# Two of twelve products with C per phase on GpSimd, and the small-argument logarithm by its remainder, in a GRU plus selective-scan kernel

## The chip, the cores and the metric

The kernel runs on one core of a Trainium2 chip. The metric is the time of the whole program on the device in microseconds (us), as the median of several runs; lower is better. A core has TensorE (PE), VectorE (DVE), ScalarE (ACT), GpSimd (POOL) and SyncE (SP, which here only issues DMAs). Each engine works through its own list of instructions in order, and they meet at semaphores.

## The reference, cut to what matters

The input is 32 images of 14 x 14 positions (T = 196) and 384 channels. A group norm and a GRU over the 196 positions come first, then a group norm and a selective scan in four directions:

```python
dts, Bs, Cs = jnp.split(x_dbl, [R, R + N], axis=2)        # N = 16 states
dts = jax.nn.softplus(einsum(dts, dt_projs_w) + dt_projs_b)
dA = jnp.exp(d_t[..., None] * As)                          # per channel and state
h = h * dA + (d_t * u_t)[..., None] * B_t[:, :, None, :]
y = jnp.einsum('bkcn,bkn->bkc', h, C_t)
```

The four y are added, normalised over the channels, gated with silu(z) and projected.

## The kernel before, in words

The GRU and the projections of all images fill the first 1,020 us. The change touches only what follows: a loop over 16 pairs of images (`PAIRS`), in each of which four directions (the phases `st` = 0 to 3, which the change's title calls phases and the prediction stages) are done one after the other. A stage has twelve groups `g`. A group holds a block of 128 partitions x 784 elements (`GC`): four runs of 196 positions, each for one state and a part of the channels. One group passes through all engines:

- GpSimd, `drive` (L484): delta\*u times B, into one of six buffers `hb` (`RING` = 6), so group g uses the buffer of group g - 6 and waits until that one was summed (the semaphore `reduced`). B comes by DMA, replicated over the partitions, in three chunks of four groups.
- ScalarE, `decays` (L950): exp(delta\*A) in two halves into three PSUM banks (`DEC` = 3), so a half waits for the scan three halves before.
- VectorE, `scan` (L767): two scan instructions of 392 elements, in place in `hb`; then `read_out` (L782): the product with C, in place. C lies in PSUM banks 3 and 4, put there by TensorE.
- TensorE, `spread` (L1229): four matmuls that replicate the C rows of a group into banks 3 and 4; `reduce` (L1237): matmuls with the identity that add the group into the sum over the states, banks 5 and 6.

In TensorE's list (`pair`, L1302) iteration g waits for the product of group g - 1, spreads C of group g and reduces group g - 1; projections for the next stage and the tail of the image pair before are hung on behind: `dt_proj` at g = 0 and 2, a wait for ScalarE's reading of it (`dt_read`) at g = 3 and 4, `centre_hw` at (0,3), `centre_wh` at (0,4), `var` at (1,4), `out_proj` with `residual` at (3,3) and (3,5), `bc_proj` at g = 8 and 9.

In GpSimd's list (`pair`, L513) drive(g) is followed at g = 4 by `resid_of` (L448), at g = 8 by `low_parts` (L454), and at g = 10 and 11 by the five steps of `delta_step` (L460), which make delta and delta\*u of the next stage. In stage 2 `normed` (L498) stands behind drive(4), ahead of `resid_of`, and `gated` (L502) behind drive(7): both belong to the pair of images before. ScalarE's `mid_parts` (L922, at g = 3) waits for `resid_of`, and its `affine` (L992, at (2,2)) for `normed`.

The softplus is max(x,0) + log(1+e) with e = exp(-|x|). Before, for e under 0.022 a series takes the place of what the plain logarithm loses: ScalarE makes it by a square and a copy, GpSimd by two products and differences, and VectorE's `choose` (L790, once a stage, after group 8) picks it. The order of all lists is written out by hand; no planner is at work. SyncE issues the loads, each behind the wait that frees its target (`pair`, L341).

Of the kernel before, what the change touches and what calls it, by code (L numbers as in the profile page):

```python
# [39 lines left out]
CHUNK = 16 * T  # L40
EPS = 1e-5
UNROLL = 32
A_LOG_MAX = 88.72
SMALL = 0.022
# [5 lines left out]
def build(nc, x_seq, x_pair, wx, wh, bx, bh, wp, win, par, xproj, dtproj, wout, out):  # L50
# [4 lines left out]
    b_by_image = nc.dram_tensor("b_by_image", [K4, 2, N, T], F32)  # L55

    with ExitStack() as ctx:
# [18 lines left out]
        ident = sb("ident", [128, 128])  # L76
        sel = sb("sel", [96, N, 3, 128], BF16)
# [15 lines left out]
        series_bias = sb("series_bias", [128, 1])  # L93
# [40 lines left out]
        def carve(cols):  # L134
# [19 lines left out]
        poly = carve(TC)  # L154
# [26 lines left out]
            "dt_ready", "dt_read", "soft_step", "series_step", "choice_ready", "log_ready", "delta_ready", "du_ready",  # L181
# [6 lines left out]
            "b_spilled", "b_chunk0", "b_chunk1", "b_chunk2", "skipped")}  # L188
# [20 lines left out]
        def group_aps(g):  # L209

            if g < 8:
                return (lambda a: a[:, 0:T2].unsqueeze(1).broadcast_to([128, 2, T2]),
                        lambda bank: ps[:, bank:bank + 2, 0:T2],
                        lambda a: a.rearrange("p (m c) -> p m c", m=2))
            return (lambda a: a[:, T2:TC].unsqueeze(1).unsqueeze(1).broadcast_to([128, 2, 2, T]),
                    lambda bank: ps[:, bank:bank + 2, 0:T2].rearrange("p m (q t) -> p m q t", q=2),
                    lambda a: a.rearrange("p (m q t) -> p m q t", m=2, q=2))

# [12 lines left out]
        def _(sp):  # L231
# [65 lines left out]
            def spill_b(P, k):  # L297
# [3 lines left out]
                sp.dma_start(b_by_image[k].rearrange("i n t -> (i n) t"), xdbl[0:2 * N, 0:T]).then_inc(s["b_spilled"], 16)  # L301

# [14 lines left out]

            spill_b(0, 0)
            for j in range(3):
                spread_b(0, 0, j, True)  # L320
            spill_xc(PAIRS - 1)
# [19 lines left out]
            def pair(i, head, last):  # L341
                for st in range(K4):
# [5 lines left out]
                    if st == 1 and not last:  # L348
                        next_x(i)
                    if ahead:  # L350
                        spread_b(P1, k1, 1)
                    if st == 3 and not head:
# [17 lines left out]
        def _(pool):  # L370
# [89 lines left out]
            def delta_step(n, P, k, b, early=False):  # L460

                if n == 0:
                    pool.wait_ge(s["soft_step"], P * 4 + 3)
                    pool.tensor_tensor(poly, poly, soft, ALU.mult).then_inc(s["series_step"], 1)  # L464
                elif n == 1:
                    pool.wait_ge(s["soft_step"], P * 4 + 4)
                    pool.wait_ge(s["series_step"], P * 2 + 1)
                    pool.tensor_tensor(poly, poly, lnp, ALU.subtract).then_inc(s["series_step"], 1)  # L468
                elif n == 2:
                    pool.wait_ge(s["series_step"], P * 2 + 2)  # L470
                    pool.tensor_tensor(lnp, lnp, relu, ALU.add).then_inc(s["log_ready"], 1)  # L471
                elif n == 3:
                    pool.wait_ge(s["choice_ready"], P + 1)
# [3 lines left out]
                    pool.tensor_tensor(delta[b], lnp, poly, ALU.add).then_inc(s["delta_ready"], 1)  # L477
# [6 lines left out]
            def drive(P, st, g, G, early):  # L484
# [7 lines left out]
                if not early:  # L492
                    pool.wait_ge(s["reduced"], G - (RING - 1))
# [12 lines left out]

            pool.wait_ge(s["xc_loaded"], 16)
            resid_of(0, 0)
            low_parts(0, 0)
            for n in range(5):  # L510
                delta_step(n, 0, 0, 0, True)

            def pair(i, head, last):  # L513
                for st in range(K4):
# [3 lines left out]
                    for g in range(GRP):  # L518
                        drive(P, st, g, i * (K4 * GRP) + (st * GRP + g), head and st * GRP + g < RING)
                        if (st, g) == (2, 4) and not head:  # L520
# [10 lines left out]
                        if g >= 10:  # L531
                            for n in (0, 1, 2) if g == 10 else (3, 4):
# [11 lines left out]
        def _(dve):  # L544
            dve.memset(series_bias[:, :], -(3.0 ** 0.5) / 4.0).then_inc(s["const_ready"], 1)
# [123 lines left out]
            dve.wait_ge(s["const_ready"], 2)  # L669
# [112 lines left out]
            def read_out(st, g, G):  # L782
# [4 lines left out]
                dve.wait_ge(s["c_ready"], G + 1)  # L787
                dve.tensor_tensor(h, h, bank(3), ALU.mult).then_inc(s["readout_ready"], 1)  # L788

            def choose(P):  # L790

                dve.wait_ge(s["series_step"], P * 2 + 2)
                dve.scalar_tensor_tensor(poly, soft, SMALL, poly, ALU.is_lt, ALU.mult  # L793
                    ).then_inc(s["choice_ready"], 1)

            def pair(i, head, last):
                for st in range(K4):
                    for g in range(GRP):
# [7 lines left out]
            choose(0)  # L806
# [7 lines left out]
        def _(act):  # L814
# [98 lines left out]
            def read_bc(P, st, first=False):  # L913
                act.wait_ge(s["bc_ready"], P * 2 + 2)
                if not first:
                    act.wait_ge(s["dt_ready"], P * 2)
                    act.wait_ge(s["resid_ready"], P)
                    act.wait_ge(s["b_spilled"], P * 48)
                act.activation(xdbl[:, :], ps[:, 7, 0:T2], ACT.Copy).then_inc(s["xdbl_ready"], 1)
# [17 lines left out]
            def series(P, part):  # L937

                if part == 0:
# [3 lines left out]
                    act.activation(poly, soft, ACT.Square, scale=3.0 ** -0.5, bias=series_bias[:, 0:1]  # L943
                        ).then_inc(s["soft_step"], 1)
# [143 lines left out]
        def _(pe):  # L1088
# [39 lines left out]
            pe.wait_ge(s["const_ready"], 2)  # L1128
# [108 lines left out]
            def reduce(st, g):  # L1237
# [4 lines left out]
                opens, closes = st % 2 == 0 and g in (0, 8), st % 2 == 1 and g in (7, 11)  # L1242
# [59 lines left out]
            def pair(i, head, last):  # L1302
                for st in range(K4):
# [3 lines left out]
                    for g in range(GRP):  # L1307
# [4 lines left out]
                        if not opening:  # L1312
                            pe.wait_ge(s["readout_ready"], G)
                        spread(g, st)
                        if not opening:
# [4 lines left out]
                            reduce(*((st, g - 1) if g else ((st - 1) % K4, GRP - 1)))  # L1320

# [55 lines left out]
            pe.wait_ge(s["readout_ready"], PAIRS * K4 * GRP)  # L1377
# [60 lines left out]
```

## Time and profile before

| | |
|---|---|
| median of 3 runs | 3240.07 us (3240.0 to 3241.2) |
| the profiled execution's own time | 3240.27 us |
| its span | 3238.3 us |
| PE busy | 2779.2 us, 86% |
| DVE busy | 2672.7 us, 83% |
| POOL busy | 2243.0 us, 69% |
| ACT busy | 1824.2 us, 56% |
| DMA, mean over the span | 119 GB/s |

Shares over the span mix two programs, the GRU and the scan loop. The loop on VectorE runs from 1022.79 us to 3203.93 us, 2181.14 us; in it DVE is busy for 2141.79 us (98%), POOL for 1952.29 (90%), PE for 1816.78 (83%) and ACT for 1589.99 (73%). A timeline row gives the start, the duration, the engine, the line, and how many instructions were merged in it; what stands in brackets is the idle time before it and who ended it. A row's duration includes its way out of the engine's pipeline, so the distance between two starts is what one instruction costs its engine.

### The profile page before, as it was taken

How to read it: one execution, taken by the hardware profiler on the slowest of the kernel's cores; microseconds unless marked ns; L12 is line 12 of the kernel's file. 1: busy time of each engine (PE TensorE's matmuls, PEld its weight loads, DVE VectorE, ACT ScalarE, POOL GpSimd, SP SyncE). 2: the span in 40 equal slices, each digit the busy share in tenths (PEclk: the TensorE clock that was granted, in tenths of full speed). 3: DMA queues.
4: the chain of work that ended last, by engine and by line, in shares of the span. 5: the costliest groups of instructions: out<-in, count | busy, mean ns of one | idle time of the engine just before them, and what ended most of it. 6: DMA issues, size and time to landing. Idle time of an engine off the chain costs nothing.

```text
span 3238.3 us, 101526 instructions
## 1 busy us (share of the span) xinstructions
PE 2779.2 (86%) x39496; PEld 2070.2 (64%) x39496; DVE 2672.7 (83%) x4226; ACT 1824.2 (56%) x3872; POOL 2243.0 (69%) x1878
## 2 busy tenths in 40 slices
PE   4999999999996788888888888888888888888886
PEld 4999999986664555555555555565555655656554
DVE  6444444445776999999999999999999999999995
ACT  1111111112224677777777777777777777777773
POOL 5333333320005989989899898888989898898983
PEclk9999999999997999999999999999999999999999
DMA  5000000002334555545545555455454554555541
GB/s 199 0 0 0 0 0 0 0 5 97 112 112 140 156 156 153 153 156 149 177 140 163 159 144 169 141 160 174 134 170 149 157 163 140 162 161 155 162 146 46
DMA packets 57085, 385.29 MB, mean 119 GB/s; under 512 B 10100, under 2 KB 15060, under 8 KB 31700
## 3 DMA queue, kind: packets, MB, share of 16 engines
q1 hardware_dynamic: 57044, 384.79, 38.8%
q8 instruction: 20, 0.33, 0.0%
q14 instruction: 21, 0.17, 0.0%
HBM read 352.64 MB, written 32.11 MB: 119 GB/s over the span
## 4 chain that ended last, share of the span: by engine, by line
DVE 30%; PE 25%; issue 23%; POOL 16%; ACT 3%; DMA 1%; DVEq 1%; POOLq 0%; SPq 0%; ACTq 0%
DVE arena L776 15%; PE ps L1112 10%; PE ps L1121 9%; POOL arena L495 9%; DVE arena L779 9%; PE ps L1108 2%; DVE arena L793 1%; DVE conv_out L203 1%; POOL arena L471 1%; POOL arena L464 1%; POOL arena L468 1%; DVEq L773 1%; DMA x_in<-x_pair 1%; POOL arena L477 1%; POOL arena L482 1%
## 5 line engine op out<-in xcount | busy, mean ns | idle before, releaser
L1244 PE MATMUL ps<-arena,ident 128*128 128x392 f32 (+1 forms) x4096 | 1163.0, 417 | 0.9 <-DVE arena L788 0.9
L963 ACT ACTIVATE ps<-arena,abias,a 128x390 f32<-128x390 f32 x1024 | 690.0, 677 | 317.4 <-DVE arena L779 179.8
L788 DVE TENSOR_TENSOR arena<-arena,ps 128x784 f32<-128x784 f32 x768 | 745.7, 971 | 38.2 <-PE ps L1234 12.8
L1244 PEld LDWEIGHTS ps<-arena,ident 128*128 128x128 f32 x4096 | 682.8, 191 | 143.9 <-DVE arena L788 1.2
L776 DVE TENSOR_TENSOR_SCAN arena<-ps,arena 128x392 f32<-128x392 f32 x768 | 702.6, 956 | 7.4 <-POOL arena L495 6.3
L779 DVE TENSOR_TENSOR_SCAN arena<-ps,arena 128x392 f32<-128x392 f32 x768 | 702.6, 956 | 0.0
L1234 PE MATMUL ps<-arena,sel 96*128 96x196 bf16 x3072 | 391.6, 250 | 355.7 <-DVE arena L788 355.7
L1234 PEld LDWEIGHTS ps<-arena,sel 96*128 96x128 bf16 x3072 | 227.5, 97 | 665.0 <-DVE arena L788 630.7
L967 ACT ACTIVATE ps<-arena,abias,a 128x195 f32<-128x195 f32 x1024 | 477.7, 505 | 254.2 <-DVE arena L776 139.8
L495 POOL TENSOR_TENSOR arena<-arena 128x784 f32<-128x784 f32 x256 | 472.7, 1851 | 102.6 <-PE ps L1244 97.3
L495 POOL TENSOR_TENSOR arena<-arena,wx_sb 128x784 f32<-128x784 f32 x256 | 465.4, 1850 | 14.4 <-POOL arena L482 13.7
L495 POOL TENSOR_TENSOR arena<-arena,wh_sb 128x784 f32<-128x784 f32 x256 | 467.9, 1850 | 0.0
L422 POOL COPY arena<-h_t 128x96 f32 x196 | 71.6, 365 | 421.5 <-DVE h_t L667 421.5
L1112 PE MATMUL ps<-wx_sb,x_cur 128*32 128x96 f32 x14112 | 333.2, 248 | 0.0
L1121 PE MATMUL ps<-wh_sb,h_t 128*32 128x96 f32 x14112 | 330.6, 247 | 0.0
L1112 PEld LDWEIGHTS ps<-wx_sb,x_cur 128*32 128x32 f32 x14112 | 290.9, 110 | 23.1 <-issue 0.2
L652 DVE TENSOR_TENSOR rh<-r_gate,ps 128x96 f32<-128x96 f32 x196 | 49.8, 254 | 308.6 <-PE ps L1121 308.6
L1121 PEld LDWEIGHTS ps<-wh_sb,h_t 128*32 128x32 f32 x14112 | 296.9, 110 | 4.9
L843 ACT ACTIVATE r_gate<-ps 128x96 f32<-128x96 f32 x196 | 49.0, 250 | 394.0 <-PE ps L1121 394.0
L439 POOL TENSOR_TENSOR grstd<-gsum,neg_half 128x6 f32<-128x6 f32 x16 | 21.2, 1323 | 240.3 <-DVE gsum L723 240.3
L1214 PE MATMUL ps<-arena,bc_w 128*128 128x196 f32 x768 | 150.0, 332 | 1.5 <-ACT arena L935 0.8
L1214 PEld LDWEIGHTS ps<-arena,bc_w 128*128 128x128 f32 x768 | 133.6, 192 | 19.6 <-ACT arena L935 1.4
(175 smaller groups left out, 3295.4 us busy)
## 6 DMA issues: line engine op xcount, KB each, us to landing
wx_sb<-b_by_state SPq DMA_DIRECT2D x64, 1568.0 KB, 6.3
wh_sb<-b_by_state SPq DMA_DIRECT2D x64, 1568.0 KB, 6.3
arena<-b_by_image SPq DMA_DIRECT2D x128, 784.0 KB, 9.1
arena<-x_seq SPq DMA_DIRECT2D x4, 2352.0 KB, 15.9
x_in<-x_pair SPq DMA_DIRECT2D x16, 588.0 KB, 4.2
x_dram<-x SPq DMA_DIRECT2D x16, 588.0 KB, 2.8
x<-x_dram SPq DMA_DIRECT2D x16, 588.0 KB, 10.0
out<-xhat SPq DMA_DIRECT2D x16, 588.0 KB, 2.8
```

Source lines behind the costliest of these rows:

```text
L422: pool.tensor_copy(tok(t), h_t[:, p, :]).then_inc(s["hist_done"], 1)
L495: pool.tensor_tensor(view(hb[(st * GRP + g) % RING]), dux(du[b]), view(src), ALU.mult).then_inc(s["drive_ready"], 1)
L776: dve.tensor_tensor_scan(h, ps[:, bank, 0:HALF_C], h, 0.0, ALU.mult, ALU.add).then_inc(s["scan_done"], 1)
L779: dve.tensor_tensor_scan(h[:, ::-1], ps[:, bank, 1:HALF_C + 1][:, ::-1], h[:, ::-1], 0.0, ALU.mult, ALU.add).then_inc(s["scan_done"], 1)
L788: dve.tensor_tensor(h, h, bank(3), ALU.mult).then_inc(s["readout_ready"], 1)
L963: ins = act.activation(r, src, ACT.Exp, scale=a01[:, c:c + 1], bias=abias01[:, c:c + 1])
L967: ins = act.activation(r[:, m, :], delta[b][:, T2 + lo:T2 + lo + T - 1], ACT.Exp, scale=a2[:, c:c + 1], bias=abias2[:, c:c + 1])
L1112: mm = pe.matmul(ps[32 * j:32 * j + 32, bank + p, 0:CJ], x_cur[:, p, 32 * k:32 * k + 32], wx_sb[:, k, j, lo:lo + CJ], start=False, stop=False)
L1121: mm = pe.matmul(ps[32 * j:32 * j + 32, bank + p, at:at + CJ], h_t[:, 1 - p, 32 * k:32 * k + 32], wh_sb[:, k, j, lo:lo + CJ], start=False, ...
L1214: mm = pe.matmul(ps[:, 7, bc * T:(bc + 1) * T], bc_w[:, k, bc, tile, :], x[:, tile * T:(tile + 1) * T], start=(tile == 0), stop=(tile == 2))
L1234: mm = pe.matmul(ps[:, 3 + m // 2, m % 2 * T:m % 2 * T + T], sel[:, n, kind, :], rhs, start=True, stop=True)
L1244: mm = pe.matmul(ps[:, 5 if g < 8 else 6, 0:cols], ident[:, :], h[:, m * cols:(m + 1) * cols], start=(opens and m == 0), stop=(closes and ...
```

## The change

Groups 2 and 6 of every stage lose VectorE's `read_out`; GpSimd multiplies them instead (`pool_read`), three drives after their own, with a copy of C that DMA wrote to DRAM and spread over the partitions (`spread_c`). TensorE doesn't spread C for them, and reduces them two iterations later than before: at g = 5 and 9. The order of the reductions becomes 0, 1, 3, 4, 2, 5, 7, 8, 6, 9, 10, 11, and `drive` counts `reduced` by that order. The softplus takes its logarithm of w = 1 + e as rounded, and adds the remainder e - (w - 1): two copies and a Ln on ScalarE, four steps on GpSimd, none on VectorE. The diff, cut to its core:

```diff
+POOL_READS = (2, 6)
+DVE_READS = GRP - len(POOL_READS)
+READ_LEAD = 3
+BEHIND = 2
@@ sync, spill_b
+                for q, g in enumerate(POOL_READS):
+                    for img in range(2):
+                        sp.dma_start(c_by_state[k][q, :, img, :], xdbl[N * img + 2 * g:N * img + 2 * g + 2, T:T2]
+                                     ).then_inc(s["c_spilled"], 16)
+            def spread_c(P, k, first=False):
+                sp.wait_ge(s["c_spilled"], (P + 1) * (32 * len(POOL_READS)))
+                if not first:
+                    sp.wait_ge(s["pool_read"], P * len(POOL_READS))
+                rows = c_by_state[k].rearrange("q n i t -> (q n i t)").unsqueeze(0)
+                sp.dma_start(c_chunk[:, :], rows.broadcast_to([128, len(POOL_READS) * GC])).then_inc(s["c_chunk_in"], 16)
@@ sync, pair
                     if ahead:
                         spread_b(P1, k1, 1)
+                    if ahead and max(POOL_READS) + READ_LEAD >= 8:
+                        spread_c(P1, k1)
@@ gpsimd, delta_step
                 if n == 0:
                     pool.wait_ge(s["soft_step"], P * 4 + 3)
-                    pool.tensor_tensor(poly, poly, soft, ALU.mult).then_inc(s["series_step"], 1)
+                    pool.tensor_tensor(rest, soft, rest, ALU.subtract).then_inc(s["rest_ready"], 1)
                 elif n == 1:
-                    pool.tensor_tensor(poly, poly, lnp, ALU.subtract).then_inc(s["series_step"], 1)
+                    pool.tensor_tensor(lnp, lnp, rest, ALU.add).then_inc(s["log_ready"], 1)
                 elif n == 2:
-                    pool.tensor_tensor(lnp, lnp, relu, ALU.add).then_inc(s["log_ready"], 1)
-                elif n == 3:
-                    pool.wait_ge(s["choice_ready"], P + 1)
-                    pool.tensor_tensor(delta[b], lnp, poly, ALU.add).then_inc(s["delta_ready"], 1)
+                    pool.tensor_tensor(delta[b], lnp, relu, ALU.add).then_inc(s["delta_ready"], 1)
@@ gpsimd, drive
-                    pool.wait_ge(s["reduced"], G - (RING - 1))
+                    before = st * GRP + g - RING
+                    place = before // GRP * GRP + ORDER.index(before % GRP)
+                    pool.wait_ge(s["reduced"], G - (st * GRP + g) + (place + 1))
@@ gpsimd
+            def pool_read(P, st, g, G):
+                _, _, view = group_aps(g)
+                h = view(hb[(st * GRP + g) % RING])
+                q = POOL_READS.index(g)
+                if q == 0:
+                    pool.wait_ge(s["c_chunk_in"], P * 16 + 16)
+                pool.wait_ge(s["scan_done"], G * 2 + 2)
+                pool.tensor_tensor(h, h, view(c_chunk[:, q * GC:(q + 1) * GC]), ALU.mult).then_inc(s["pool_read"], 1)
@@ gpsimd, pair
                         drive(P, st, g, ...)
+                        if g - READ_LEAD in POOL_READS:
+                            pool_read(P, st, g - READ_LEAD, ...)
-                            for n in (0, 1, 2) if g == 10 else (3, 4):
+                            for n in (0, 1) if g == 10 else (2, 3):
@@ vector, pair
-                        read_out(st, g, G)
-                        if g == 8 and not (last and st == K4 - 1):
-                            choose(i * K4 + (st + 1))
+                        if g not in POOL_READS:
+                            read_out(i * K4 + st, st, g, G)
@@ scalar, series
-                    act.activation(poly, soft, ACT.Square, scale=3.0 ** -0.5, bias=series_bias[:, 0:1]
+                    act.activation(lnp, soft, ACT.Copy, bias=1.0).then_inc(s["soft_step"], 1)
-                    act.activation(poly, poly, ACT.Copy, bias=13.0 / 16.0).then_inc(s["soft_step"], 1)
-                    act.activation(lnp, soft, ACT.Ln, bias=1.0).then_inc(s["soft_step"], 1)
+                    act.activation(rest, lnp, ACT.Copy, bias=-1.0).then_inc(s["soft_step"], 1)
+                    act.wait_ge(s["soft_step"], P * 4 + 3)
+                    act.activation(lnp, lnp, ACT.Ln).then_inc(s["soft_step"], 1)
@@ tensor, pair
-                            pe.wait_ge(s["readout_ready"], G)
-                        spread(g, st)
-                        if not opening:
+                            pe.wait_ge(s["readout_ready"], P * DVE_READS + dve_reads_before(g))
+                        if g not in POOL_READS:
+                            spread(g, st)
+                        if not opening and (g - 1) % GRP not in POOL_READS:
                             reduce(*((st, g - 1) if g else ((st - 1) % K4, GRP - 1)))
+                        if g - 1 - BEHIND in POOL_READS:
+                            r = g - 1 - BEHIND
+                            pe.wait_ge(s["pool_read"], P * len(POOL_READS) + (POOL_READS.index(r) + 1))
+                            reduce(st, r)
```

## Rows read from the trace of the kernel before

**Rows 1.** Windows, stages 1 to 0 of one pair: busy time of each engine.

```profile
1874.71:2011.14 136.43, 114.58 (x584) 79.53 (x584) 133.94 (x150) 100.22 (x192) 122.87 (x79) 1.00 0.52 156
```

**Rows 2.** Waits of the loop: engine and line, releaser, us in total, times, longest.

```profile
POOL arena L495 <- PE ps L1244: 97.3, 89, 2.0
```

**Rows 3.** Timeline of DVE: scans, products with C, the choice L793.

```profile
1874.71 1.83 DVE L779 TENSOR_TENSOR_SCAN arena<-ps,arena 128x392 f32<-128x392 f32 x2
1876.58 0.97 DVE L788 TENSOR_TENSOR arena<-arena,ps 128x784 f32<-128x784 f32 x1
1877.47 1.83 DVE L779 TENSOR_TENSOR_SCAN arena<-ps,arena 128x392 f32<-128x392 f32 x2
...
1933.19 1.40 DVE L793 SCALAR_TENSOR_TENSOR arena<-arena 128x588 f32<-128x588 f32 x1
...
1956.22 0.97 DVE L788 TENSOR_TENSOR arena<-arena,ps 128x784 f32<-128x784 f32 x1 [0.61 <-PE ps L1234]
...
1968.11 0.77 DVE L793 SCALAR_TENSOR_TENSOR arena<-arena 128x588 f32<-128x588 f32 x1
```

**Rows 4.** Timeline of POOL, stage 2 and the first drives of stage 3.

```profile
1887.80 1.87 POOL L495 TENSOR_TENSOR arena<-arena 128x784 f32<-128x784 f32 x1 [0.27 <-PE ps L1244]
...
1912.72 1.42 POOL L500 TENSOR_TENSOR arena<-arena 128x588 f32<-128x588 f32 x1
1914.11 0.54 POOL L451 TENSOR_TENSOR arena<-arena 96x196 f32<-96x196 f32 x1
...
1921.43 1.85 POOL L495 TENSOR_TENSOR arena<-arena 128x784 f32<-128x784 f32 x1
1923.36 0.55 POOL L456 TENSOR_TENSOR arena<-arena 32x196 bf16<-32x196 f32 x1
1924.07 3.67 POOL L495 TENSOR_TENSOR arena<-arena 128x784 f32<-128x784 f32 x2 [0.16 <-POOL arena L456]
1927.69 1.44 POOL L464 TENSOR_TENSOR arena<-arena 128x588 f32<-128x588 f32 x1
1929.21 1.44 POOL L468 TENSOR_TENSOR arena<-arena 128x588 f32<-128x588 f32 x1
...
1934.75 1.43 POOL L477 TENSOR_TENSOR arena<-arena 128x588 f32<-128x588 f32 x1 [0.79 <-DVE arena L793]
1936.35 1.43 POOL L482 TENSOR_TENSOR arena<-arena 128x588 f32<-128x588 f32 x1 [0.16 <-POOL arena L477]
1938.02 7.27 POOL L495 TENSOR_TENSOR arena<-arena,wx_sb 128x784 f32<-128x784 f32 x4 [0.24 <-POOL arena L482]
```

**Rows 5.** Timeline of PE: spread, reduce, and extras at g = 3 and 4.

```profile
1885.87 0.51 PE L1234 MATMUL ps<-arena,sel 96*128 96x196 bf16 x4 [0.90 <-DVE arena L788]
1886.21 1.51 PE L1244 MATMUL ps<-arena,ident 128*128 128x392 f32 x4
1887.56 0.82 PE L1259 MATMUL ps<-arena,avg 128*128 128x392 f32 x2
...
1953.52 0.93 PE L1292 MATMUL ps<-arena,wout 128*128 128x392 f32 x2 [0.50 <-ACT arena L935]
...
1955.61 0.50 PE L1234 MATMUL ps<-arena,sel 96*128 96x196 bf16 x4
...
1987.90 0.92 PE L1259 MATMUL ps<-arena,centring 128*128 128x392 f32 x2 [0.59 <-ACT arena L935]
...
1989.32 0.50 PE L1234 MATMUL ps<-arena,sel 96*128 96x196 bf16 x4
```

**Rows 6.** Timeline of ACT, stage 2, groups 2 to 4.

```profile
1914.18 1.16 ACT L996 ACTIVATE arena<-arena,par 128x392 f32<-128x392 f32 x2 [0.34 <-POOL arena L500]
1915.24 1.26 ACT L963 ACTIVATE ps<-arena,abias,a 128x390 f32<-128x390 f32 x2
1916.53 0.36 ACT L924 ACTIVATE arena<-arena 32x196 bf16<-32x196 f32 x1
...
1918.93 0.42 ACT L935 ACTIVATE arena<-ps,par 128x196 f32<-128x196 f32 x1
```

More of the change, by code:

```diff
@@ L76, in build @@
         ident = sb("ident", [128, 128])
+        c_chunk = sb("c_chunk", [128, len(POOL_READS) * GC])
         sel = sb("sel", [96, N, 3, 128], BF16)
@@ L153, in build @@
         lnp = carve(TC)
-        poly = carve(TC)
+        rest = carve(TC)
         z_fin = carve(TC)
@@ L180, in build @@
             "xc_loaded", "xt_ready", "bc_ready", "xdbl_ready", "resid_ready", "mid_ready", "parts_ready",
-            "dt_ready", "dt_read", "soft_step", "series_step", "choice_ready", "log_ready", "delta_ready", "du_ready",
+            "dt_ready", "dt_read", "soft_step", "rest_ready", "log_ready", "delta_ready", "du_ready",
             "b_ready", "c_ready", "decay_ready", "drive_ready", "scan_done", "readout_ready", "reduced",
@@ L186, in build @@
             "oproj_ready", "o_ready", "out_stored", "fin_z", "fin_x1",
-            "b_spilled", "b_chunk0", "b_chunk1", "b_chunk2", "skipped")}
+            "b_spilled", "b_chunk0", "b_chunk1", "b_chunk2", "skipped",
+            "c_spilled", "c_chunk_in", "pool_read")}
         convs = ((pad01, conv01_out, 2 * H + 1, par01, s["conv01_step"]), (pad2, conv2_out, H, par2, s["conv2_step"]))
@@ L217, in group_aps, with dve_reads_before, reduce_order @@
                     lambda a: a.rearrange("p (m q t) -> p m q t", m=2, q=2))
+        def dve_reads_before(g):
+            return g - sum(r < g for r in POOL_READS)
+        def reduce_order():
+            order, late = [], []
+            for g in range(GRP):
+                if g in POOL_READS:
+                    late.append(g)
+                else:
+                    order.append(g)
+                order += [r for r in late if r + BEHIND == g]
+            return order
+        ORDER = reduce_order()
         def half_cols(hf):
@@ L320, in _ @@
                 spread_b(0, 0, j, True)
+            spread_c(0, 0, True)
             spill_xc(PAIRS - 1)
@@ L349, in pair @@
                         next_x(i)
+                    if ahead and max(POOL_READS) + READ_LEAD < 8:
+                        spread_c(P1, k1)
                     if ahead:
                         spread_b(P1, k1, 1)
+                    if ahead and max(POOL_READS) + READ_LEAD >= 8:
+                        spread_c(P1, k1)
                     if st == 3 and not head:
@@ L509, in _ @@
             low_parts(0, 0)
-            for n in range(5):
+            for n in range(4):
                 delta_step(n, 0, 0, 0, True)
@@ L918, in read_bc @@
                     act.wait_ge(s["b_spilled"], P * 48)
+                    act.wait_ge(s["c_spilled"], P * (32 * len(POOL_READS)))
                 act.activation(xdbl[:, :], ps[:, 7, 0:T2], ACT.Copy).then_inc(s["xdbl_ready"], 1)
@@ L1127, in _ @@
             pe.wait_ge(s["bias_step"], 17)
-            pe.wait_ge(s["const_ready"], 2)
+            pe.wait_ge(s["const_ready"], 1)
             pe.wait_ge(s["x_ready"], 1)
@@ L1241, in reduce @@
                 cols = GC // runs
-                opens, closes = st % 2 == 0 and g in (0, 8), st % 2 == 1 and g in (7, 11)
+                tile = [r for r in ORDER if (r < 8) == (g < 8)]
+                opens, closes = st % 2 == 0 and g == tile[0], st % 2 == 1 and g == tile[-1]
                 for m in range(runs):
```

22 lines of the change are left out of this document (7 added, 15 removed).

## The prediction

> **What bounds the kernel now.** I read first the windows over one pair of images [rows 1]: of 136.43 us VectorE is busy for 133.94, and GpSimd, for all that its share of the whole span is 69%, for 122.87. So there is one bound and one engine 13.6 us a pair behind it, and this change moves work from the first to the second. The waits [rows 2] show what GpSimd's slack is: it waits 97.3 us for reductions, that is, for a buffer of the ring; it runs ahead until all six are full. The timeline of VectorE [rows 3] has no gaps: a group costs 2.76 us (1874.71 to 1877.47), two scans and a product with C. With that picture the change looks like a clean gain. It has to be checked against the waits that close a circle, so I then read the timelines of POOL, PE and ACT [rows 4 to 6] and follow one stage through them.
>
> **VectorE's part.** A product starts 1.87 after its group and the next group 0.89 later. Without the product the next scan follows the second scan at once; one scan's start comes after half of 1.83 plus, some 0.88, so a group without a product costs 1.76: 1.00 saved, twice a stage. The choice goes: it costs 0.68 to 1.32 (its 0.77 or 1.40 less the overlap of 0.08), say 0.8. VectorE's stage falls from 34.1 (a quarter of 136.43) by 2.8 to 31.3.
>
> **GpSimd's part.** Drives cost 1.81 each, as (7.27 - 1.85) / 3 [rows 4]. The new product is the same form, 784 elements, two inputs in SBUF; only its second operand isn't repeated. The nearest row without a repeated operand is a delta step, 1.43 for 588 elements, 1.91 scaled to 784: I take 1.81, bound 1.91. Below 1.81 nothing speaks. Delta steps: 1.52 where one waits for the other, 1.39 before a drive (1912.72 to 1914.11, the same form), 1.60, and 1.67 from the last to the drive (1936.35 to 1938.02 [rows 4]). Stage, start to start: 14 x 1.81 = 25.34; `resid_of` 0.51 (0.54 less overlap); drive 8 to `low_parts` 0.12 more than a drive, `low_parts` 0.66 to 0.71; four delta steps 1.52 + 1.39 + 1.60 + 1.67 = 6.18. Sum 32.8; in stage 2 `normed` and `gated` add 2 x 1.39. The mean is 33.5, under today's 34.1 by only 0.6. GpSimd is now the busier of the two, so it no longer runs ahead: VectorE waits for drive 0 at the end of each stage and starts scanning as that drive ends.
>
> **The circle.** Drive 8 writes the buffer of group 2. It needs `reduced` at 5, and the order of reductions is 0, 1, 3, 4, 2: group 2 is summed after group 4, and group 4 is summed when VectorE has multiplied it. Let 0 be the start of scan 0. Groups 0, 1, 3 and 4 cost 2.76 each, group 2 1.76; the product of group 4 starts at 11.9 and ends at 12.85. TensorE starts the spread of iteration 5 0.06 after it (a product ended at 1885.81, the spread starts at 1885.87), 0.34 later reduce(4), 1.35 later (1886.21 to 1887.56) reduce(2), which takes 1.51: 16.11 [rows 5]. Drive 8 starts 0.08 later (reduce ended 1887.72, drive 1887.80 [rows 4, 5]): 16.19. GpSimd on its own was ready for it at about 14.9: seven drives less the 0.1 they overlap the start (12.6), `resid_of` 0.5, the product of group 2 1.8. So it stands for 1.3. From drive 8 to the end of drive 0 of the next stage nothing else can help: 1.93 + 0.66 + drive 9 1.81 + product 6 1.81 + drive 10 1.81 + 1.52 + 1.39 + drive 11 1.81 + 1.60 + 1.67 + 1.84 = 17.85. Scan 0 starts some 0.06 later. The circle is 34.1 long: already all that a stage costs today. The other late reduction, group 6, is free at about 26.3, and drive 0 of the next stage comes after 32: no wait. That is the floor; now what stands on the circle in each stage of a pair with a predecessor.
>
> **TensorE, iterations 3 and 4.** ScalarE's `mid_parts` waits for `resid_of`. Today GpSimd is far ahead; in the circle it comes after drive 4, at 7.7. From `mid_parts` to the end of the last softplus read is 2.82 (1916.53 to 1918.93 + 0.42 [rows 6]), so `dt_read` is there at 10.5, and TensorE, which waits for it in iteration 3, is 0.4 behind the product of group 3 (10.1). What is hung on behind this wait comes on top: today it is 1.42 for `centre_hw` (1987.90 to 1989.32) and 2.09 for `out_proj` and `residual` (1953.52 to 1955.61 [rows 5]). After that come spread(4), without which product 4 can't start (in [rows 3] one started 0.61 after its spread, having waited 0.61), reduce(3), the extra of iteration 4, and the chain above.
> - Stage 0: 10.57 + 1.42 = 11.99, product 4 from 12.6, reduce(3) from 12.33 to 13.67, `centre_wh` 1.33 (the 1.42 of `centre_hw`, whose first matmul took 0.92 after its wait where one without a wait took 0.82 [rows 5], less 0.09), spread(5) at 15.0, reduce(2) over at 18.2. Drive 8 at 18.3: +2.1.
> - Stage 1: spread(4) 10.57, reduce(3), `var` 1.33 (the same shapes) to 13.6, then 0.34 + 1.35 + 1.51: drive 8 at 16.9: +0.7.
> - Stage 3: 10.57 + 2.09 = 12.66, product 4 from 13.3 to 14.24, PE free at 14.35, reduce(2) over at 17.55: drive 8 at 17.6: +1.4.
>
> **Stage 2, ScalarE.** `affine` stands in ScalarE's list ahead of the decays of group 3 and waits for `normed`, which comes behind drive 4. Today that wait is 0.34 [rows 6]. In the circle `normed` ends at 7.15 + 1.42 = 8.6; `affine` costs 1.06 (1914.18 to 1915.24), the first decay of group 3 is there at 10.4, and VectorE wanted it at 7.3. It stands for 3.1, and product 4 ends at 16.0. `dt_read` comes at 8.61 + 5.17 = 13.8 (1914.18 to 1919.35 [rows 6]) and is hidden. Drive 8 at 19.3: +3.1; `normed` and `gated` themselves are hidden in it (GpSimd would be ready at 17.7).
>
> **The sum.** Four stages: 4 x 34.1 + 2.1 + 0.7 + 3.1 + 1.4 = 143.7 against 136.43, +7.3 a pair. Fourteen middle pairs: +102. The first pair has no predecessor and none of these extras, before or after: 4 x 34.1 against about as much, 0. The last pair: stages 0 to 2 together 108.2 against 102.1, +6; its last stage feeds no other, so VectorE's two products count (-2.0), the choice isn't in it, late spread +0.8: -1. Ahead of scan 0 one delta step and the choice go, -2.5. Together +105: the profiled execution's own 3240.3 (0.2 above the median) becomes 3345.
>
> **What I cost at nothing.** ScalarE's series: two copies instead of a square and a copy, hidden in its idle 36 us a pair [rows 1]. Five DMAs more on SP's queue a stage: the spread of C waits for product 6, at about 21 of a stage, and is wanted at 9.5 of the next, 22 us later; spread_b(2), behind it, waits for drive 11 anyway. The wait of `read_bc` for `c_spilled` is a whole stage old. If C came late, each us would be one on GpSimd, that is 64 a us.
>
> **A rule weighed.** The choice, which reads two SBUF inputs on VectorE, took 0.77 once and 1.40 once, the second beside a drive; products with C, one input from PSUM, take 0.97 whatever GpSimd does [rows 3]. The Trainium skill ("SBUF — State Buffer", Who interferes with whom) says just this: a VectorE instruction with two SBUF inputs is blocked by a GpSimd one that reads SBUF, one with a single SBUF input is not. The trace agrees, and by it the change costs VectorE nothing. But another page of the Trainium skill ("Perfetto Trace Analysis", Optimizing Scalar/DVE Operations) warns that offloading between these two "might not help", since they share a read port. The fifth case below is what that would do here.
>
> **The cases and their chances.** A change under 0.2% (6.5 us) can't be told from none here.
> 1. The circle with its extras: 3345, own range 3285 to 3400. Chance 0.60.
> 2. The other side: the wait of drive 8 doesn't bind, because reduce(2) is done by 14.9 of the stage; GpSimd's own path of 33.5 rules. 64 x (33.5 - 34.1) = -36: 3204. For it: drive 8 stands for only 1.3 in a plain stage; against it: each part of it is a row. It decides as soon as group 2 is reduced ahead of group 4. Chance 0.10.
> 3. The circle without extras (ScalarE and TensorE find their time elsewhere): 34.1 a stage, stage 2 at 35.6 by GpSimd's path: 3241 to 3264. Chance 0.10: 0.03 same, 0.06 slower, 0.01 faster.
> 4. More stalls than I followed: each late spread holds a product, a further 1.0 a stage: 3409. Chance 0.14.
> 5. Two products a stage on GpSimd shut VectorE out for their length, 2 x 1.85: 31.3 + 3.7 = 35.0, 64 x 0.9 = +59: 3299. The drives, of the same form, do nothing of the kind to scans (0.92 each beside them [rows 3]). Chance 0.02.
> 6. VectorE stays the bound: 64 x -2.8 = -179: 3061. It would need GpSimd under 31.3 a stage, against 32.8 counted. Chance 0.04.
>
> Faster 0.15, same 0.03, slower 0.82. The range, 3225 to 3425, leaves out cases 2 and 6 and the end of case 4.
>
> **What would show it.** VectorE should be busy for about 122 of 143 us a pair (133.94 less eight products of 0.97 and four choices of about 0.9), its largest waits those for drive 0 and drive 11, for the decays of group 3 in stage 2, and for the spreads of groups 4 and 5. POOL should wait for PE once a stage, at drive 8, 1.3 us in a plain stage and 2 to 3.5 in others, and for nothing else of weight. The stage lengths should be near 36.2, 34.8, 37.2 and 35.5 for stages 0 to 3. If drive 8 doesn't wait, the forecast is wrong; if the stage lengths are all alike, the extras are.

## The result, and the profile after

The changed kernel takes 3389.26 us (median of 4 runs, 3386.27 to 3391.3) against 3240.03 us: ratio 1.046, 95% interval 1.0442 to 1.0478. It is 149 us slower, where 105 were forecast; the time lies in the range given, and the direction is right.

Section 1 of the page of the changed kernel, and its clock line:

```profile
PE 2826.5 (84%) x38984; PEld 2129.6 (63%) x38984; DVE 2501.0 (74%) x4033; ACT 1814.3 (54%) x3872; POOL 2376.3 (70%) x1942
...
PEclk9999999999988989898998989989899998999899
```

VectorE does 172 us less work and GpSimd 133 more, as the change says, and no engine is at its limit any longer. New is the last line, TensorE's clock. Before, the granted clock over the loop was 1.00; now it falls to 8 in many slices and is 0.93 over the loop (1055 to 3350 us).

The windows over stages 0 to 3 of one pair (the same columns as in [rows 1]: us, busy PE, PEld, DVE, ACT, POOL, granted clock, DMA share):

```profile
1890.87:2037.52 146.65, 119.02 (x554) 84.02 (x552) 123.16 (x137) 99.58 (x192) 131.22 (x83) 0.92 0.55 167
```

143.7 was forecast where [rows 1] had 136.43. VectorE's 123.16 is near the forecast 122: it idles for 23 us. The waits of the loop (engine and line, who ended the wait, us in total, times, longest; smaller and unrelated rows are left out), where [rows 2] had 97.3 us for GpSimd:

```profile
POOL arena L533 <- PE ps L1287: 194.2, 77, 4.2
...
DVE arena L837 <- PE ps L1276: 116.2, 113, 2.9
...
PE ps L1276 <- ACT arena L977: 100.4, 29, 5.6
...
DVE arena L828 <- POOL arena L533: 75.8, 46, 2.1
...
DVE arena L825 <- POOL arena L533: 62.2, 31, 2.1
...
ACT arena L1038 <- POOL arena L538: 44.8, 15, 3.2
...
DVE arena L825 <- ACT ps L1005: 41.2, 15, 3.1
```

L533 is `drive`, L1287 `reduce`, L825 and L828 are the scans, L837 the product on VectorE, L1276 `spread`, L977 ScalarE's reading that sets `dt_read`, L1005 `decays`, L538 `normed`, L1038 `affine`. The first row looks like more of [rows 2], and is the opposite. Before, GpSimd waited because it had filled the ring. Now nearly all of it is one wait a stage, at drive 8, and VectorE waits for GpSimd in turn at the stage's end. The timeline of POOL shows it in stages 1, 2 and 3 (scan 0 at 1927.20, 1962.10 and 2001.91; L553 is the new product `pool_read`):

```profile
1936.55 1.85 POOL L553 TENSOR_TENSOR arena<-arena,c_chunk 128x784 f32<-128x784 f32 x1
1938.36 3.67 POOL L533 TENSOR_TENSOR arena<-arena,wh_sb 128x784 f32<-128x784 f32 x2
1944.03 1.85 POOL L533 TENSOR_TENSOR arena<-arena 128x784 f32<-128x784 f32 x1 [2.00 <-PE ps L1287]
...
1960.12 7.26 POOL L533 TENSOR_TENSOR arena<-arena,wx_sb 128x784 f32<-128x784 f32 x4 [0.23 <-POOL arena L518]
...
1983.87 1.85 POOL L533 TENSOR_TENSOR arena<-arena 128x784 f32<-128x784 f32 x1 [4.19 <-PE ps L1287]
...
2019.42 1.85 POOL L533 TENSOR_TENSOR arena<-arena 128x784 f32<-128x784 f32 x1 [2.70 <-PE ps L1287]
```

Counted from scan 0, drive 8 starts at 16.83, 21.77 and 17.51, and in the next stage 0 at 18.26 (2055.78 after a scan 0 at 2037.52). Forecast were 16.9, 19.3, 17.6 and 18.3: three agree within 0.1 us, stage 2 is 2.5 late. From drive 8 to the next scan 0 it is 1962.10 - 1944.03 = 18.07, forecast 17.85 + 0.06. The stages' means over the pairs with a predecessor, from scan 0 to the next scan 0 on VectorE, in us:

| stage | before | forecast | after | lowest to highest |
|---|---|---|---|---|
| 0 | 34.14 | 36.2 | 36.44 | 36.02 to 36.85 |
| 1 | 33.71 | 34.8 | 35.40 | 34.59 to 36.59 |
| 2 | 34.30 | 37.2 | 39.21 | 38.19 to 39.83 |
| 3 | 34.28 | 35.5 | 35.59 | 35.37 to 35.63 |

What made stage 2 longer still is in the timelines of ScalarE and TensorE and in the granted clock of the window 1974 to 1984:

```profile
1970.62 1.16 ACT L1038 ACTIVATE arena<-arena,par 128x392 f32<-128x392 f32 x2 [2.98 <-POOL arena L538]
```

```profile
1970.40 0.50 PE L1276 MATMUL ps<-arena,sel 96*128 96x196 bf16 x4
1975.92 0.83 PE L1276 MATMUL ps<-arena,sel 96*128 96x196 bf16 x4 [5.02 <-ACT arena L977]
1976.55 2.87 PE L1287 MATMUL ps<-arena,ident 128*128 128x392 f32 x4
1979.21 0.86 PE L1276 MATMUL ps<-arena,sel 96*128 96x196 bf16 x4
1979.86 5.25 PE L1287 MATMUL ps<-arena,ident 128*128 128x392 f32 x12
```

```profile
1974.00:1984.00 10.00, 8.08 (x22) 4.78 (x23) 9.54 (x12) 9.19 (x17) 5.81 (x5) 0.66 0.44 161
```

TensorE stood for 5.02 us waiting for `dt_read`, which waited for `affine`, which waited for `normed`. When it went on, a reduction took 2.66 us from start to start (1976.55 to 1979.21) instead of the 1.35 of [rows 5]: it ran at 1.2 GHz, not 2.4. The granted clock is 0.50 from 1975.3 to 1982.1, and two reductions and two spreads of that time lie on the circle. The forecast followed the wait and not the lower clock behind it.

The same makes two kinds of stage 1. Ten of fourteen last 34.9 to 36.2 us, four last 36.6, and the four are those in which a stretch at the lower clock lies some 12 to 15 us after scan 0, where the circle passes through TensorE. Here are two of them, each with the window 12 us after its scan 0:

```profile
2073.84:2108.72 34.88, 27.66 (x135) 19.59 (x134) 30.83 (x35) 24.36 (x47) 32.10 (x21) 0.95 0.55 172
2085.80:2089.20 3.40, 3.40 (x17) 2.35 (x16) 3.15 (x5) 3.12 (x6) 2.85 (x2) 1.00 0.01 2
2219.37:2255.96 36.59, 27.77 (x134) 20.12 (x133) 30.83 (x35) 24.51 (x47) 32.12 (x21) 0.94 0.52 161
2231.30:2234.60 3.30, 3.30 (x9) 2.15 (x8) 2.90 (x4) 3.02 (x6) 2.88 (x2) 0.50 0.00 0
```

Both stages have a granted clock of about 0.95 as a whole: what counts is where in the stage the slow stretch falls.

### The profile page after: what moved, and what is told of

Same layout as the page of the kernel before. It is cut to its first block, busy times and chain, and to the rows that moved or that the text cites. A ratio compares the mean times of both kernels' runs of the same rounds, so it can differ in the third digit from the quotient of the medians.

```text
span 3384.5 us, 100690 instructions
## 1 busy us (share of the span) xinstructions
PE 2826.5 (84%) x38984; PEld 2129.6 (63%) x38984; DVE 2501.0 (74%) x4033; ACT 1814.3 (54%) x3872; POOL 2376.3 (70%) x1942
## 4 chain that ended last, share of the span: by engine, by line
PE 37%; POOL 32%; issue 19%; DVE 8%; ACT 2%; DMA 1%; POOLq 1%; DVEq 0%; SPq 0%; ACTq 0%
POOL arena L533 19%; PE ps L1154 9%; PE ps L1163 9%; PE ps L1287 9%; POOL arena L553 5%; PE ps L1276 2%; POOL arena L504 2%; DVE arena L825 2%; POOL arena L508 2%; PE ps L1150 2%; DVE arena L837 1%; DVE conv_out L209 1%; DVE arena L828 1%; POOL arena L518 1%; PE ps L1256 1%
## 5 line engine op out<-in xcount | busy, mean ns | idle before, releaser
L1287 PE MATMUL ps<-arena,ident 128*128 128x392 f32 (+1 forms) x4096 | 1236.4, 445 | 23.2 <-DVE arena L837 22.9
L1005 ACT ACTIVATE ps<-arena,abias,a 128x390 f32<-128x390 f32 x1024 | 675.7, 674 | 463.0 <-DVE arena L828 189.1
L1287 PEld LDWEIGHTS ps<-arena,ident 128*128 128x128 f32 x4096 | 741.7, 202 | 286.0 <-DVE arena L837 74.5
L825 DVE TENSOR_TENSOR_SCAN arena<-ps,arena 128x392 f32<-128x392 f32 x768 | 698.3, 956 | 119.1 <-POOL arena L533 77.9
L837 DVE TENSOR_TENSOR arena<-arena,ps 128x784 f32<-128x784 f32 x640 | 621.6, 971 | 181.0 <-PE ps L1276 118.5
L828 DVE TENSOR_TENSOR_SCAN arena<-ps,arena 128x392 f32<-128x392 f32 x768 | 696.9, 956 | 78.7 <-POOL arena L533 76.8
L1276 PE MATMUL ps<-arena,sel 96*128 96x196 bf16 x2560 | 341.4, 258 | 402.9 <-DVE arena L837 302.4
L533 POOL TENSOR_TENSOR arena<-arena 128x784 f32<-128x784 f32 x256 | 473.5, 1850 | 202.2 <-PE ps L1287 192.8
L1276 PEld LDWEIGHTS ps<-arena,sel 96*128 96x128 bf16 x2560 | 216.5, 101 | 569.4 <-DVE arena L837 501.1
L533 POOL TENSOR_TENSOR arena<-arena,wx_sb 128x784 f32<-128x784 f32 x256 | 464.2, 1844 | 13.6 <-POOL arena L518 9.8
L533 POOL TENSOR_TENSOR arena<-arena,wh_sb 128x784 f32<-128x784 f32 x256 | 470.3, 1848 | 0.0
L553 POOL TENSOR_TENSOR arena<-arena,c_chunk 128x784 f32<-128x784 f32 x128 | 236.4, 1847 | 0.0
```

The source lines that it names most:

```text
L533: pool.tensor_tensor(view(hb[(st * GRP + g) % RING]), dux(du[b]), view(src), ALU.mult).then_inc(s["drive_ready"], 1)
L553: pool.tensor_tensor(h, h, view(c_chunk[:, q * GC:(q + 1) * GC]), ALU.mult).then_inc(s["pool_read"], 1)
L825: dve.tensor_tensor_scan(h, ps[:, bank, 0:HALF_C], h, 0.0, ALU.mult, ALU.add).then_inc(s["scan_done"], 1)
L828: dve.tensor_tensor_scan(h[:, ::-1], ps[:, bank, 1:HALF_C + 1][:, ::-1], h[:, ::-1], 0.0, ALU.mult, ALU.add).then_inc(s["scan_done"], 1)
L1005: ins = act.activation(r, src, ACT.Exp, scale=a01[:, c:c + 1], bias=abias01[:, c:c + 1])
L1276: mm = pe.matmul(ps[:, 3 + m // 2, m % 2 * T:m % 2 * T + T], sel[:, n, kind, :], rhs, start=True, stop=True)
```

## Experiments

All ratios are to the kernel before, timed on the same chip, with their 95% interval. Where two kernels were timed on different chips, their difference is taken from the ratios.

**The late reduction.** One constant is changed: groups 2 and 6 are reduced one iteration after that of a product on VectorE, not two.

```diff
-BEHIND = 2
+BEHIND = 1
```

> The change with BEHIND = 1: TensorE reduces group 2 behind group 3 and group 6 behind group 7, so drive 8 no longer hangs on the product of group 4. All the work of the change stays. Circle theory: drive 8 waits under 0.5 us in a plain stage, stages near 33.1, 32.8, 36 to 38 and 33.8 us, together about 3225 us (3205 to 3270). Rival 1, GpSimd's own 33 to 34 us of work with some contention is what costs: 3350 to 3390, as the change. Rival 2, the lower clock of TensorE comes first and everything follows from it: stays over 3330.

Measured: 3279.87 us, 1.0129 (1.0112 to 1.0146): some 107 of the 149 us come from this constant alone. GpSimd's wait for TensorE:

```profile
POOL arena L533 <- PE ps L1287: 79.9, 57, 2.7
```

Stage 1 falls from 35.40 to 32.31 (about 32.8 was expected), stage 0 to 34.88; stages 2 and 3 stay at 37.35 and 35.49. So the circle is right, rivals 1 and 2 are not, and I took too little for what is left: 10 us over my range. What is left is ScalarE's wait for `normed` and TensorE's lower clock at iterations 3 and 4, which now delay the reduction of group 2 behind group 3. The clock's price can be read here: in the looped pairs stage 0 lasts 34.1 to 34.2 us the eight times that TensorE keeps its full clock, and 35.7 to 35.8 the six times that a stretch at the lower one falls between 10 and 15 us after its scan 0. Stage 3 lasts 35.4 to 35.6 with such a stretch and 33.95 the one time that it has none.

**The ring.** Two more buffers, one new and one in weights that are no longer used. Everything of the change stays.

```diff
-RING = 6
+RING = 8
...
-        hb = [carve(GC) for _ in range(RING)]
+        hb_more = sb("hb_more", [128, GC])
+        wp_cols = wp_sb[:, :, :].rearrange("p a b -> p (a b)")
+        hb = [carve(GC) for _ in range(6)] + [hb_more[:, 0:GC], wp_cols[:, 0:GC]]
```

> The change with a ring of eight buffers instead of six: drive 8 writes the buffer of group 0 and no longer waits for the late reduction of group 2. Everything else is as in the change. Circle theory: drive 8 never waits, GpSimd's own path of 32.8 us a stage (35.6 in stage 2) rules, about 3205 us (3195 to 3235). Rival, the stages are long because of TensorE's and ScalarE's late spreads and lower clock whatever the ring: over 3300 us.

Measured: 3232.79 us, 0.9984 (0.9974 to 0.9994): 154 us less than the change. The waits of POOL (L555 is the product, L535 `drive`; rows between are left out):

```profile
POOL arena L555 <- DVE arena L830: 21.2, 29, 1.1
...
POOL arena L535 <- PE ps L1289: 2.7, 11, 0.2
```

194.2 us of waiting for reductions are 2.7. The late reductions are still there, TensorE still idles, the same products are on GpSimd: what cost the time was GpSimd waiting for a buffer, above all at drive 8. GpSimd's path doesn't rule alone, though: stages of 34.68, 32.35, 36.38 and 33.15, 28 us over my middle value and inside the range.

**The clock.** 22 matmuls (44 in the profile's count) into columns of bank 6 that nobody reads, in TensorE's iteration 3 of stage 2; they add nothing to the result.

```diff
+                            if (st, g) == (2, 3):
+                                for w in range(22):
+                                    pe.matmul(ps[:, 6, T2:512], ident[:, :], ident[:, 0:512 - T2], start=True, stop=True)
                             if g in (3, 4) and ahead:
```

> The change, with 22 matmuls into unused columns of PSUM bank 6 in TensorE's iteration 3 of stage 2, where it stood idle for 5 us waiting for dt_read; they do no useful work. If the lower clock after that idle time is what made stage 2 last 38.2 to 39.8 us instead of 37.2, stage 2 falls to about 37.3 and the granted clock stays at 1.00 over groups 4 and 5: some 30 us less than the change, 3359 us. If the clock only accompanies a stall that has another cause, 3389 us and stage 2 as long as before. If the matmuls themselves push the spread of group 4 back, slower than 3389.

Measured: 3375.17 us, 1.0422 (1.0405 to 1.0440). TensorE in stage 2 (L1377 are the added matmuls), and the window over groups 4 and 5:

```profile
2113.54 5.09 PE L1377 MATMUL ps<-ident 128*128 128x120 f32 x44
2118.65 0.51 PE L1276 MATMUL ps<-arena,sel 96*128 96x196 bf16 x4
2118.99 1.51 PE L1287 MATMUL ps<-arena,ident 128*128 128x392 f32 x4
```

```profile
2118.00:2128.00 10.00, 9.29 (x42) 5.64 (x40) 9.17 (x12) 9.20 (x18) 8.03 (x6) 1.00 0.44 161
```

The clock stays at 1.00, the reduction takes its 1.51 again, and stage 2 lasts 37.38 (37.14 to 37.42) where 37.2 had been forecast without a word on the clock. That is the missing term of stage 2. But only 12 to 14 of some 28 us show in the total, and of the 30 expected: stage 0 went from 36.44 to 37.08, up to 38.03 where the change had at most 36.85. There TensorE also idles, and the clock isn't the same in every pair: stage 0 lasts 38.0 in the six looped pairs in which the lower clock falls 11.3 to 15 us after its scan 0, and 36.3 to 36.9 in the other eight.

**`normed` earlier.**

```diff
-                        if (st, g) == (2, 4) and not head:
+                        if (st, g) == (2, 0) and not head:
                             normed(i - 1)
```

> The change, with normed (the normalising product of the pair before) behind drive 0 of stage 2 instead of drive 4, so that ScalarE's affine and the decays of group 3 wait for nothing. Circle theory: stage 2 falls from 39.7 to GpSimd's own path, 35.6 to 36.5; 15 x 3.5 = 52 us less than the change, 3337 us (3325 to 3350). Rival, stage 2 is long because of normed and gated as work on GpSimd: no change, 3389 us.

Measured: median 3379.94 us (3361 to 3385), 1.0422 (1.0387 to 1.0457), far over the 3325 to 3350 expected. Stage 2 fell to 36.61, near what was expected, so the wait of `affine` was the reason of its length. The total didn't follow: stage 0 rose to 37.53 and stage 1 to 36.14. Neither of the two expectations had this. Two stages 0 of this kernel, each with the window 11 or 12 us after its scan 0:

```profile
2036.52:2072.84 36.32, 29.53 (x152) 21.88 (x150) 30.72 (x34) 25.05 (x49) 32.10 (x21) 1.00 0.58 180
2047.90:2051.30 3.40, 3.40 (x18) 2.49 (x17) 2.94 (x4) 2.79 (x5) 3.40 (x2) 1.00 0.34 144
2179.95:2217.96 38.01, 31.22 (x152) 22.80 (x150) 30.73 (x34) 25.16 (x49) 32.11 (x21) 0.96 0.55 173
2192.00:2195.40 3.40, 3.40 (x10) 2.09 (x9) 2.63 (x4) 2.48 (x5) 2.77 (x2) 0.50 0.16 66
```

Eleven of the fourteen looped stages 0 are of the second kind, where the change had none: the stretch at the lower clock, which cost little elsewhere in the stage, has moved onto the circle and costs 1.7 us. Mending a stage shifts where it falls in the next ones. Which idle time decides that, these runs don't tell.

**The logarithm alone.** `POOL_READS = ()`, with nothing of C by DMA.

> The new logarithm alone: all twelve products with C stay on VectorE, nothing of C goes by DMA. Circle theory: VectorE is the bound again and loses only the choice (0.68 to 1.33 us a stage, say 0.8), so 64 x 0.8 + 2.5 = 54 us under before: 3187 us. Rival, the new logarithm is itself what made the change slow (its copies and own waits on ScalarE put the series late): not under 3240, and over 3300 if it is the main cause.

Measured: 3235.45 us, 0.9991 (0.9982 to 1.0001): neither of the two expectations. The choice is gone and the gain with it. The timeline of VectorE in the loop has the place, a group of 2.86 and not 2.76 (L819 are scans, L831 the product):

```profile
1905.41 1.83 DVE L819 TENSOR_TENSOR_SCAN arena<-ps,arena 128x392 f32<-128x392 f32 x2
1907.39 0.97 DVE L831 TENSOR_TENSOR arena<-arena,ps 128x784 f32<-128x784 f32 x1
1908.27 1.83 DVE L819 TENSOR_TENSOR_SCAN arena<-ps,arena 128x392 f32<-128x392 f32 x2
```

A product starts 1.95 to 1.98 after its group, not 1.87; in the first pair, which is unrolled, it is 1.86 in this kernel too, and a stage lasts 33.03 there and 34.11 in the loop. The change also rewrote the wait for C from G + 1, which is i \* 48 + constant, to P \* 12 + constant with P = i \* 4 + st, which in the loop is made in a register. So the wait was written with 48 again, here and in TensorE's list (twelve products a stage, so `K4 * DVE_READS` is 48):

```diff
-                dve.wait_ge(s["c_ready"], P * DVE_READS + (dve_reads_before(g) + 1))
+                dve.wait_ge(s["c_ready"], P + (st * DVE_READS + dve_reads_before(g) + 1))
...
-                            read_out(i * K4 + st, st, g, G)
+                            read_out(i * (K4 * DVE_READS), st, g, G)
```

> The new logarithm alone (all products with C on VectorE), with the value of the wait for c_ready written as i * 40 + constant (here i * 48 + constant) instead of (i * 4 + st) * 12 + constant, in VectorE's and TensorE's lists. In the run of the logarithm alone a product started 1.95 to 1.98 us after its group in the loop and 1.86 in the unrolled first pair. If the two-step register arithmetic of that wait is what ate the choice's 0.8 us, the loop's stages fall from 34.1 to 33.0 us and the time from 3235 to about 3175 us (3170 to 3190). Rival, the 0.1 us has another cause (TensorE's spread, GpSimd's shorter list): no change, 3235 us.

Measured: 3184.12 us, 0.9832 (0.9815 to 0.9848), and the product starts 1.86 after the scans:

```profile
1996.52 1.83 DVE L822 TENSOR_TENSOR_SCAN arena<-ps,arena 128x392 f32<-128x392 f32 x2
1998.38 0.97 DVE L831 TENSOR_TENSOR arena<-arena,ps 128x784 f32<-128x784 f32 x1
```

51 us for one expression: 12 x 0.09 in each of the 56 looped stages is 60 at most, less what other waits hide. With it the new logarithm is worth what the prediction gave to the choice, 0.8 a stage. This kernel, with no product moved, is also what the ones below have to be measured against: of what they gain over the kernel before, it alone gains 54 us.

**The same in the change.** Two tries. The first wrote i \* 40 + constant:

> The change with the one-step form of the same waits and nothing else. On the circle stand four products (groups 0, 1, 3 and 4), 0.09 us each, where VectorE and not TensorE is the late one: 0.1 to 0.36 us a stage in stages 1 and 2, less in 0 and 3: 3375 to 3385 us. If the register arithmetic were a main cause of the slowdown: 10 x 0.09 a stage, 3335 us.

Measured: 3390.97 us, 1.0467 (1.045 to 1.0484), over the 3375 to 3385 expected; a product still starts 1.95 after its group. So it isn't the number of steps in the arithmetic. The form that works has a factor, 48, with which this list computes other waits too (G of `drive_ready`, for one); the likely reason is that such a value is in a register already, which was not looked at by itself. The second try therefore counts `c_ready` and `readout_ready` in groups, a spread or product behind a group of GpSimd's adding 2:

```diff
+        def groups_counted(g):
+
+            return 2 if g - 1 in POOL_READS else 1
...
-                dve.wait_ge(s["c_ready"], P * DVE_READS + (dve_reads_before(g) + 1))
-                dve.tensor_tensor(h, h, bank(3), ALU.mult).then_inc(s["readout_ready"], 1)
+                dve.wait_ge(s["c_ready"], G + 1)
+                dve.tensor_tensor(h, h, bank(3), ALU.mult).then_inc(s["readout_ready"], groups_counted(g))
...
-                mm.then_inc(s["c_ready"], 1)
+                mm.then_inc(s["c_ready"], groups_counted(g))
...
-                            pe.wait_ge(s["readout_ready"], P * DVE_READS + dve_reads_before(g))
+                            pe.wait_ge(s["readout_ready"], G - (1 if (g - 1) % GRP in POOL_READS else 0))
```

> The change with c_ready and readout_ready counted in groups and nothing else, which the run with i * 40 was meant to be. Four products of 0.09 us stand on the circle of a stage, and TensorE's lists of stages 0 and 3 are late for other reasons: stage 1 at 34.8 to 34.9 us, stage 2 up to 0.4 less than in the change: 3375 to 3390 us. If the waits' arithmetic were a main part of the 149 us, ten products of 0.09 in 64 stages, 3330 us.

Measured: 3391.65 us, 1.0459 (1.0441 to 1.0476), the change's time, 2 us over my range. The form works: where nothing holds it, a product starts 1.86 or 1.87 after its group again. Yet where the circle rules, 0.09 us on VectorE is nothing: the late one at iteration 5 is TensorE.

**One product on GpSimd.** `POOL_READS = (6,)`, with i \* 44 in the waits:

> The change with one product on GpSimd, that of group 6 (C for it alone by DMA, BEHIND = 2), and the one-step waits. Group 6's buffer is wanted by drive 0 of the next stage, which comes late, so no circle through a late reduction. GpSimd's path is 31.0 us a stage (33.8 in stage 2), VectorE's 33.0 - 1.0 = 32.0: bound by VectorE, at 64 x (32.1 - 34.1) - 2.5, with some stall in stage 2: 3115 us (3105 to 3150). Rival, any product on GpSimd brings the stalls with it: over 3240 us.

Measured: 3219.07 us, 0.9941 (0.9925 to 0.9958), 104 us above what I expected. Two reasons show. The 0.09 is there (i \* 44): a stage of VectorE's is 33.0. And GpSimd, ahead again, stands up to 3.4 us in its list for scan 6, with drive 10 and the delta steps behind it:

```profile
POOL arena L553 <- DVE arena L828: 77.4, 32, 3.4
POOL arena L553 <- DVE arena L825: 44.1, 31, 3.0
```

So the counted waits, `normed` behind drive 0 and `resid_of` behind drive 2 were added, and in a second kernel the product went behind drive 10 and its reduction to iteration 10:

```diff
-READ_LEAD = 3
-BEHIND = 2
+READ_LEAD = 4
+BEHIND = 3
```

> One product on GpSimd (group 6, three drives late, reduced two iterations late), normed behind drive 0 of stage 2, resid_of behind drive 2, and c_ready and readout_ready counted in groups (a spread or product that follows a group of GpSimd's adds 2), so that the waits have the form i * 48 + constant, which other waits of the list use too. In the runs with i * 40 or i * 44 a product still started 1.95 us after its group, in the run with i * 48 it started at 1.86: if sharing the register is what counts, VectorE's groups cost 2.76 again and a stage 32.1 us: 3115 to 3150 us, stages 1 under 32.5. If the wait for scan 6 holds GpSimd back as in the run before (3.4 us), stages of 32.5 to 33.5 and 3150 to 3190 us. If the arithmetic wasn't it: 3200 us or more.

> As f1_one_shared with the product of group 6 one drive later (behind drive 10) and its reduction one iteration later. If GpSimd's standing still for scan 6 binds in f1_one_shared, 0.5 to 1 us a stage less than that: 30 to 60 us faster than it. If VectorE's own 32.1 us bind there, the same time as it within 5 us.

Measured: 3176.44 us, 0.9815 (0.9795 to 0.9834), and 3162.33 us, 0.9766 (0.9750 to 0.9782). The second is the fastest kernel here, 75 us under the kernel before the change. Its gain over the first, 14 us, lies between the two expectations; it shows in stage 3, 33.71 to 32.64, and hardly anywhere else. Stages 1 are at 32.06, VectorE's own time; in stage 0 (33.0) three products stand for their spreads, 1.1 us in all, and stage 2 (33.7) is at GpSimd's own path for one product, 33.8. Its clock line:

```profile
PEclk9999999999998999999999999999999999999999
```

**The change, mended.** Eight buffers, counted waits, `normed` and `resid_of` early:

> The change with eight buffers, the waits counted in groups, normed behind drive 0 of stage 2 and resid_of behind drive 2. With the ring gone from the circle, stage 2 lasted 36.4 and stage 0 34.7 us instead of the 35.6 and 32.8 of GpSimd's own path; both moves take the waits of ScalarE out. Circle theory: stages 32.8 to 33.2, stage 2 35.6: 3185 us (3175 to 3205). If TensorE's lower clock keeps its share, 3215 to 3230.

Measured: 3203.06 us, 0.9896 (0.9879 to 0.9912), at the upper end of 3175 to 3205: stages of 34.15, 32.14, 35.33 and 32.84. GpSimd waits for no buffer in the loop and idles for 0.7 to 0.9 us a stage, most of it between steps of its own, and a pair lasts 134.28 us, where its own path is 4 x 32.8 + 2.8 = 134.0: GpSimd's list is the bound.

Beside the new logarithm alone with the cheap wait (0.9832), this is slower by 0.0064 of the time before, 21 us, and one product on GpSimd (0.9766) is faster by the same: of its 75 us, some 54 belong to the logarithm. How much of the rest is the product, and how much `normed` and `resid_of` coming early, no run separates.

## Why the prediction was right, and where it was short

- **VectorE -2.8 us a stage.** Its busy time fell by 10.8 a pair, forecast 11.4. As a path it was 0.9 too small by the runs on the waits: 0.09 for each of ten products. It made no difference here, and all the difference for the logarithm alone. The prediction read the wait's value and not what making it costs.
- **GpSimd's product at 1.81, bound 1.91.** Start to start 1.81 (1936.55 to 1938.36). Right.
- **The circle.** Shown twice, by BEHIND (107 us) and by the ring (154 us), and drive 8's start in stages 0, 1 and 3 came out within 0.1. Its floor was a little low: the first pair, whose stages have no extras, took 34.16 to 34.75 a stage where 34.1 was forecast, the two longer ones with a stretch at the lower clock 11 to 14 us in, and drive 8 stood there for 1.6 to 2.0, not 1.3.
- **TensorE's extras and ScalarE's `normed`.** Stages 0 and 3 within 0.3; VectorE's wait for the decays of group 3 is 41.2 / 15 = 2.75, forecast 3.1. Moving `normed` took 2.6 from stage 2.
- **The term that was too small: stage 2**, forecast at +3.1 over the circle, measured at +5.1 on the mean. The 1.35 of a reduction was carried from [rows 5] to a place behind 5 us of idle time, where it took 2.66; kept at full clock by the added matmuls, stage 2 lasted 37.4. With stage 1's +0.6, which is the clock again in part, and 0.3 in stages 0 and 3 this is 2.9 x 15 = 44 us, as much as the 44 that are missing. The first pair grew by 2.0 us where nothing was forecast, and scan 0 came 4.2 us sooner than before instead of 2.5: these two nearly cancel.
- **Rivals.** Of GpSimd's own path (3204) the prediction said that it decides as soon as group 2 is reduced ahead of group 4. That was too simple: the kernel in which it is (`BEHIND = 1`) took 3280, since drive 8 still waited in stages 0, 2 and 3. It took eight buffers, `normed` and `resid_of` early and cheap waits to come to 3203. VectorE shut out by GpSimd's products (3299) has no trace: products with C on VectorE took 0.97 beside 1.85 of GpSimd as before. C by DMA landed in 4.1 us (median) and nobody waited for it.

## What to carry to other kernels

When work moves to an engine with slack, count its list first, and then follow each buffer around: a ring of six hides a late reduction only as long as the engine that refills it is ahead, and this change took away the lead and the punctual reduction at once. A circle of waits is read by adding rows along it, from one start to the same start a stage later; if it is longer than the bound engine's stage, it is the new bound however idle all engines are. A slow stretch of TensorE costs most where the circle passes through it, so look at where it falls and not at the mean clock. A moved or recounted wait has a price of its own in a loop: look at the first, unrolled round beside a looped one. And when a change has two parts, time each by itself: here the logarithm, with a cheap wait, gained 54 us, and the two products lost more than that.

## What the runs showed of the hardware

- A wait whose value in a loop was i \* 40, i \* 44 or P \* 12 with P = i \* 4 + st, plus a constant, cost VectorE 0.09 us each beside one with i \* 48 (a product 1.95 after its group and not 1.86); once a group it was worth 51 us.
- TensorE, after 5.02 us without work, went on at 1.2 GHz; kept busy with 5.09 us of useless matmuls, it stayed at 2.4. Taking one such place away did not take away the whole cost: stages behind it got slower in the mean by 0.6 to 1.1 us.
- A stretch of 3.4 us at a granted clock of 0.50 cost 1.7 us where it fell on the circle's reductions (stage 0 of the kernel with `normed` early: 38.01 beside 36.32), and nothing where it fell 2.5 us after scan 0 (a stage 0 of the change, 36.33 beside 36.32 without one).
- Products with C on VectorE took 0.97 us beside GpSimd's products of 1.85, as before.
